# Perceiver layer on one core: the first context group's keys and comparisons ahead of the query's mask product

## The reference

```
q, k, v = q @ Wq.T, k @ Wk.T, v @ Wv.T
_focus(x): x = abs(where(x >= 0, x, 0.01 * x)) + 1e-6
           softmax(log(x) * focusing_factor) * mean(x)      # over 256
qh, kh = top-k sparsified per head of 16: the 11 largest stay
z_inv = qh . mean(kh) + eps;  kv = kh^T vh / n;  y = qh kv / z_inv
```

## Time and profile before

| | us |
|---|---|
| median of 3 runs | 511.24 (510.99 to 512.73) |
| profiled execution | 511.34 |
| its span, first to last instruction | 509.5 |
| VectorE busy | 451.5 |
| TensorE busy | 399.8 |
| ScalarE busy | 359.5 |
| mean granted TensorE clock | 0.916 of full speed |

### The profile page before, as it was taken

How to read it: one execution, slowest core, us unless ns; L and a number is a source line. 1 busy time by engine, 2 the same in 40 slices (tenths; PEclk the granted TensorE clock), 3 DMA queues, 4 the chain that set the end, 5 groups by cost and what they waited for, 6 DMA issues and landing times.

```text
span 509.5 us, 6004 instructions
## 1 busy us (share of the span) xinstructions
PE 399.8 (78%) x1880; PEld 305.2 (60%) x1880; DVE 451.5 (89%) x769; ACT 359.5 (71%) x943; POOL 16.1 (3%) x32
## 2 busy tenths in 40 slices
PE   2987749999979879878987993669989994546674
PEld 1876538888868767767776882557864432112232
DVE  4698999999999999999999999999796457589883
ACT  2579697999987987987977896567444348566642
POOL 3002410000000000000000000000000000000000
PEclk9998978999999999999999897879999999577757
DMA  7942001122202202202201202202000000000001
GB/s 238 361 146 82 1 1 42 42 84 83 69 16 82 84 0 84 83 9 75 82 27 57 84 0 82 82 2 82 2 0 0 1 1 0 2 0 0 22 21 41
DMA packets 27102, 27.65 MB, mean 54 GB/s; under 512 B 1216, under 2 KB 26816, under 8 KB 27072
## 3 DMA queue, kind: packets, MB, share of 16 engines
q1 hardware_dynamic: 26704, 27.27, 16.7%
q0 software_dynamic: 224, 0.01, 0.0%
q10 hardware_dynamic: 144, 0.00, 0.0%
HBM read 26.22 MB, written 1.05 MB: 54 GB/s over the span
## 4 chain that ended last, share of the span: by engine, by line
DVE 58%; PE 27%; ACT 11%; issue 3%; DMA 1%; SPq 0%; ACTq 0%
DVE focus_words L1125 6%; PE bank L738 6%; PE bank L884 6%; DVE focus_words L1111 6%; DVE mask L1183 6%; PE bank L802 3%; PE bank L926 3%; DVE sorted L1141 3%; DVE merge L1159 3%; DVE level L1135 3%; DVE level L1134 3%; DVE sorted L1142 3%; ACT focus_words L487 3%; PE bank L710 2%; DVE sorted L1055 2%
## 5 line engine op out<-in xcount | busy, mean ns | idle before, releaser
L802 PE MATMUL bank<-ctx_words,focus_words 128*128 128x257 f32 x512 | 120.3, 394 | 31.5 <-ACT focus_words L498 31.4
L738 PE MATMUL bank<-WkT,rows_T 128*128 128x256 f32 x512 | 124.2, 392 | 24.1 <-ACT rows_T L409 24.1
L802 PEld LDWEIGHTS bank<-ctx_words,focus_words 128*128 128x128 f32 x512 | 99.5, 197 | 49.8 <-ACT focus_words L498 35.0
L738 PEld LDWEIGHTS bank<-WkT,rows_T 128*128 128x128 f32 x512 | 97.2, 195 | 40.7 <-ACT rows_T L409 28.2
L487 ACT ACTIVATE focus_words<-focus_words,shift,ff 128x256 f32<-128x256 f32 x136 | 79.9, 591 | 0.6
L498 ACT ACTIVATE focus_words<-focus_words,row_scale 128x256 f32<-128x256 f32 x136 | 56.3, 504 | 30.2 <-DVE row_scale L1127 30.2
L409 ACT ACTIVATE rows_T<-bank 128x512 f32<-128x512 f32 x76 | 42.2, 599 | 19.6 <-PE bank L710 19.6
L454 ACT ACTIVATE focus_words<-bank 128x256 f32<-128x256 f32 x136 | 50.3, 384 | 6.8 <-PE bank L738 5.5
L1111 DVE SCALAR_TENSOR_TENSOR focus_words<-focus_words,key_and,key_xor 128x2048 int32<-128x2048 int32 x17 | 39.9, 2345 | 2.3 <-ACT focus_words L454 2.3
L1183 DVE TENSOR_TENSOR mask<-focus_words,fifth 128x2048 bf16<-128x2048 f32 x17 | 38.8, 2285 | 0.1
L1125 DVE TENSOR_TENSOR focus_words<-focus_words,mask 128x2048 f32<-128x2048 f32 x17 | 38.1, 2243 | 0.0
(11 more groups left out here) (181 smaller groups left out, 611.0 us busy)
## 6 DMA issues: line engine op xcount, KB each, us to landing
ctx_words<-in_ctx_dram SPq DMA_DIRECT2D x32, 512.0 KB, 3.9
ctx_words<-in_L_ffn_gate_w_dram SPq DMA_DIRECT2D x2, 1024.0 KB, 7.6
ctx_words<-in_L_ffn_up_w_dram SPq DMA_DIRECT2D x2, 1024.0 KB, 8.6
xs<-in_x_dram SPq DMA_DIRECT2D x4, 256.0 KB, 5.0
ctx_words<-in_L_ffn_down_w_dram SPq DMA_DIRECT2D x2, 512.0 KB, 9.5
ctx_words<-in_L_ffn_down_w_dram SPq DMA_DIRECT2D x1, 1024.0 KB, 4.8
out_dram<-xs SPq DMA_DIRECT2D x4, 256.0 KB, 2.2
focus_words<-in_L_attn_W_qkv_dram SPq DMA_DIRECT2D x1, 768.0 KB, 8.3
```

The lines of the kernel that those rows point to most:

```text
L738: ins = pe.matmul(proj_bank[m][:, t * D:(t + 1) * D], rows_T[:, m % 2, 2 * t + k, :], WT[:, k, :], start=(k == 0), stop=(k == KT - 1))
L802: ins = pe.matmul(sum_bank[k][:, 0:GW], expo[slot][:, t, k * P:(k + 1) * P], ctx_ring[:, s, t, :], start=(s == 0 and t == 0), stop=(s == P ...
```

## The change

On ScalarE, the last lift of group 1 moves ahead of the query's exponentials. On VectorE, the keys of group 1 are made right after the query's mask, ahead of `weight_max(2)`; the query's reciprocal, mask product and row scale move behind the comparisons of group 1, so the loop's body has the same order for n = 1 as for all other n, and the condition in it goes. No instruction is added or removed.

```
             lift(1, 2, 0)
+            lift(1, 3, 0)
             exponentials(0, -1)
-            lift(1, 3, 0)
             rows_to_sbuf(2, 2)
...
             find_fifth(-1)
             make_mask(0)
+            make_keys(1, 0)
             weight_max(2)
-            inverse_sums(0, -1)
-            apply_mask(0, -1, 1, 0)
             dve.wait_ge(w_max_taken, 3)
             dve.tensor_reduce(w_absmax[:, :], w_amax[:, :, :], AX.X, ALU.max).then_inc(absmax_ready, 1)
-            make_keys(1, 0)
...
                     compare_pairs(n)
-                    if n >= 2:
-                        inverse_sums(n - 1, s - 1)
-                        apply_mask(n - 1, s - 1, 3, 0)
+                    inverse_sums(n - 1, s - 1)
+                    apply_mask(n - 1, s - 1, 3, 0)
                     find_fifth(s)
```

## The result

| | us |
|---|---|
| before, median of 10 runs | 511.99 (510.79 to 513.82) |
| after, median of 10 runs | 515.63 (514.41 to 517.40) |
| ratio after to before, 95% interval | 1.007 (1.0047 to 1.0093) |
| profiled execution of after, its span | 517.16, 515.4 |

The change makes the kernel slower by 0.7%, some 3.6 us (the interval: 2.4 to 4.8). Six further runs of it gave 513.28 to 517.46.

The account below looks back on a forecast made before the run. VectorE was taken as the limit from 88 us on, nearly level before that with a chain through ScalarE and TensorE. Profiled 511.34 us plus 2.4 gives 513.7, less 0.10 to the median: 513.6 us, range 512.3 to 516.0.

Parts of the forecast that it names:

- The chain: Query row scale through ScalarE scaling, TensorE transposes and projection to group 1's exponentials: 2.61 us late after 0.63 us slack.
- rival C: Added TensorE idle time at the query's transposes slows the clock for group 3's projection: +4.4 to +6.2 us, 516.4 us; 10%.
- the last sign that I had set: Forecast is wrong if TensorE's granted clock differs between the traces from 53 to 66 us.
- VectorE's own gain: VectorE starts group 1's find_fifth (merge network) 2.08 us earlier: 1.86 us idle plus 0.2 us of waits.
- The query's row scale: On VectorE, ready at about 49.35 us instead of 46.19, 3.16 us later, behind group 1's keys and comparisons.
- The wait at r1: VectorE idles 4.3 us for ScalarE's exponentials ahead of group 1's reciprocal, which then stands 2.50 us later.
- the keys of group 2: VectorE waits 0.3 us there for ScalarE's lift, which ends at 59.32 us instead of 56.71.
- r2: Group 2's reciprocal on VectorE: 2.61 us late, or 2.10 us if ScalarE wins back half a microsecond.
- No reserve behind 88 us: VectorE sets the pace almost without idle time from 88 us, so earlier delay reaches the end almost one for one.
- The baseline: Whole kernel before: profiled execution of 511.34 us, noise some 0.7 us, three runs spanning 510.99 to 512.73 us.
- Rival A: VectorE's idle gap ahead of the query's reciprocal is simply filled: 2.08 us faster, 509.2 us; 6%.
- Rival B: ScalarE's work is late but wins the delay back before 88 us: no change, 511.3 us; 6%.

Follow-up runs that it names:

- e3_warm: Changed kernel plus unused identity transposes keeping TensorE busy before the query's transposes and the projections of groups 3 and 4: 512.99 us.
- after_again: The changed kernel, unaltered, run again for a second profile: median 516.64 us, profiled execution 513.28 us.
- e6: Changed kernel with ScalarE's order of before, so only VectorE's part of the change remains: 521.72 us.
- e7: Changed kernel with the query's transposes and qT copies moved later, and group 1's logarithms and a group 2 lift ahead of the query's scaling: 509.39 us.
- e8: Kernel before with only the query's transposes and qT copies moved out of the way of group 3's projection: 510.46 us.
- e9: Kernel before with unused transposes on TensorE, 18 ahead of the projection of group 3 and 36 ahead of group 4's: 510.56 us.
- e2_keys_in_gap: Kernel before with the lift moved as in the change, but only group 1's keys put ahead of the query's reciprocal on VectorE: 512.32 us.

## Why the prediction was right, and where its size was off

The time lies inside the range (512.3 to 516.0) and in the direction of the forecast; the size was +3.6 us against a forecast of +2.4. The chain was forecast well, but that the time came out inside the range owes something to luck. My own forecast went up to +3.5, and the measured +3.6 lies just above; the range reached further, to 516.0, only for the nearer half of rival C, to which I gave 10%. And by the last sign that I had set, a granted clock that differs between 53 and 66 us, the forecast fails for the profiled execution (0.65 against 1.00) and holds for the second profile (1.00).

- **VectorE's own gain.** Forecast 2.08 us at the merge network of group 1; the profile shows 13.94 - 11.87 = 2.07.
- **The query's row scale, 3.16 us late.** Scaling started 12.04 us behind the mask instead of 8.88: 3.16. My list of steps gives this number; the sentence that explains it (4.7 us of work against 1.86 and 0.2) gives only 2.64, since it leaves out the small reduction at L1195, which also moved ahead of the product: 2.27 + 2.3 + 0.46 - 1.86 = 3.17.
- **The chain, 2.61 us late.** In the second profile of after the logarithms of group 1 start 55.71 - 37.29 = 18.42 us behind the mask, before 53.34 - 37.56 = 15.78: 2.64 us. The wait at r1 is 4.19 us (forecast 4.3) and r1 stands 32.84 - 30.30 = 2.54 us later (forecast 2.50); the keys of group 2 waited 0.26 (forecast 0.3). At r2 the forecast was 2.10 to 2.61; e3_warm, with the projection of group 4 at the full clock too, shows 51.54 - 49.48 = 2.06, after_again 2.68. e6 confirms the path with a larger dose, e7 and e8 by taking it away.
- **No reserve behind 88 us.** As forecast, to the end of the context loop: from r2 to the last scaling it is 245.57 us after and 245.58 before. Behind the loop after is 0.7 us shorter, which is within the 1.6 us by which that stretch varies over the profiles; what makes it vary stays open.
- **The size: TensorE's clock.** This is the term that failed. I gave rival C (the idle stretch added ahead of the query's transposes brings the clock down) 10% and 4.4 to 6.2 us. In the profiled execution of after it happened: r2 is 55.24 - 49.48 = 5.76 us late. The excess over the clean chain at r1 is 36.55 - 32.84 = 3.71 us: about 1.1 in the query's transposes and qT copies (57.90 - 38.42 = 19.48 us from mask to logarithms against 18.42) and the rest in the projection of group 3, with 3.78 us for 1.99 in its first eight matmuls. Of 16 runs of after only one (513.28) lies where the clean chain puts it over the lower group. That C or a part of it is the usual case is read from these times; a profile shows it for one run only.
- **The baseline.** I took the profiled execution (511.34) as typical. It is of the lower group; over half of before's runs stand 2.5 us higher (513.61 against 511.07, the medians of the groups), and the one of them that was profiled has slow projections of groups 2 and 3. I read the spread of three runs, 510.99 to 512.73, as noise. By these profiles the same clock term was at work in before, and the change made it more frequent. With extra transposes in both, the change costs 2.4 us (e3 against e9); against before as it runs it costs 3.6.
- **Rival A** (the gap is filled, 2 us faster) fell by e2_keys_in_gap. Its premise holds only where the other chain has slack: in e7 against e8 the same order gains 2.00 us at r1. **Rival B** fell: the delay stays in both profiles of after.

That the slow clock follows from the added idle stretch is shown for the sum (e3_warm fills the stretches, and the median goes from 515.63 to 512.99), not for the single stretch: the query's gap alone was not filled. Nor does the gap decide it alone: in the second profile of after TensorE idles 2.69 us for the scaled rows, then 3.07, and the projection runs at the full clock. Why e3_warm keeps two loose groups (512.0 to 512.7, 513.3 to 514.3) stays open.

## What to carry to other kernels

Before work is moved into an idle gap of the busiest engine, follow the result that it overtakes: if another engine's chain waits for that result and stands level with the busy engine, the gap only moves to the next meeting point, and the delay of the overtaken result, less what slack its chain has, is paid (here 2.6 of 3.16 us, before any clock loss). Take the overtaken result off that chain first (here the query's transposes and copies; e7 is at 0.9938 of before, 0.9916 to 0.996, and 6.2 us under the change's median), and then the same reordering pays (2.00 us at r1, 1.07 in the median, e7 against e8).

Idle time of TensorE can have a price even where it looks free: behind an idle stretch of 3.07 us the first eight matmuls of a projection on the path took 1.99 us in some executions and up to 3.78 in others. If repeated runs of a kernel fall into two groups, profile one of each before taking either as the baseline.

## What the runs showed of the hardware

The kernel alone on one core has two groups of times, 2.5 us apart, with the same code and data. The profiles of one execution of each differ in two projections, both behind idle stretches of the same 3.07 us: that of group 3 took 1.99 us for eight matmuls at a granted clock of 1.00 in one and 3.38 at 0.58 in the other, and that of group 2 took 5.40 us for sixteen at 0.68 and 6.65 at 0.55. In e2_keys_in_gap, behind a stretch of 3.08 us, the same sixteen took 3.72. Useless transposes ahead of the projections of groups 3 and 4 alone removed the upper group (12 runs, 509.53 to 511.44), though the projection of group 2 still took 5.41 us in the profile, and made the kernel faster by 0.36% (0.9946 to 0.9982).
